# Four engine call lists of a pipelined delta-rule layer laid out in a new order

## The chip, the cores and the metric

The kernel runs on one core of one Trainium2 chip. The metric is the device time of one execution in microseconds. The kernel before takes 4942.76 us, the median of 3 runs (4940.17 to 4954.71). All data is 32-bit floating point.

## The reference

Three layers run one after the other on x of shape (8, 256, 256): a feed-forward layer, an attention layer and a second feed-forward layer. Nearly all of the time is the attention layer (16 heads, 4 keys per token, chunks of 64 tokens in the reference). For every head and chunk:

```python
w = bg[..., None] * kg
M = tril(einsum(k * decay, w), k=-1)              # keys against keys
rhs = vg - einsum('bhtid,bhdv->bhtiv', k * exp(G), S)
u = solve_triangular(M, rhs, lower=True, unit_diagonal=True)
o = scale * (q * exp(G) @ S + einsum(q * decay, w) @ u)
S_new = exp(glast) * S + einsum('bhtid,bhtiv->bhdv', kdec, u)
```

Here q, k and v come from projections of the normalised x, a causal convolution with four taps and a silu; q is normalised over its channels, k through its lengths. G is the running sum of a softplus of a low-rank projection. The output is normalised by its root mean square, gated and projected back.

## The kernel before, in words

The attention layer is cut into 64 steps: 4 blocks of 512 tokens (two sequences each) times 16 heads. The kernel cuts the recurrence into chunks of 32 tokens, so a step has 16 chunks, eight for each of the two sequences. It is a software pipeline written out by hand. A loop variable p runs over periods, and in one period every engine does parts of up to four steps: projections and convolutions of step p, products and masks of step p-1, inverses and the start of the recurrence of step p-2, the rest of the recurrence and the output of step p-3. Each of TensorE (PE), VectorE (DVE), ScalarE (ACT) and GpSimd (POOL) has its own list of calls, which stands in the code in the order in which the engine executes it. Nothing plans this order at run time: an engine takes its next call, waits until the semaphores that the call names have reached their counts, and executes it. So the order of a list is the order of the queue, and a call that waits holds everything behind it.

The calls that matter, by the names in the lists (first argument: the step):

- project_k(s, b) and project_v(s, b) on PE: two 128x512 matrix products each into one of two shared banks. tap_k or tap_v on ACT copies the bank into one of three accumulators, and three calls conv_k or conv_v on DVE (m = 2, 1, 0) add the other taps from the bank and so give it free. silu_k and silu_v on ACT write the result (tiles KQ and V). The tables bank_use and acc_use say which bank or accumulator each use has, and for whose release it waits.
- levels(s, q, l) on DVE writes the scaled keys (tile X) of quarter q of a step at level l from 1 to 4; level(s, q) on POOL does level 0 (tile X0). products(s, q, l) on PE multiplies them with a stationary tile of 128x32. Levels 0 to 2 go to bank 2, levels 3 and 4 to bank 3. When the five products of a quarter are there, evacuate(s, q, 0..3) on DVE (tile Pd, lines 1661 and 1667) and keep(s, q) on ACT (tiles E and At) read them, and only then may products(s, q+1, 0) start.
- take, norm and weigh on DVE prepare the 32x32 diagonal blocks; begin and rows on POOL invert them row by row (tiles LT and LZ, lines 1998 and 2001). unfold and turn on DVE bring the result back (Zc, Ztc), place and shift on ACT lay it into Ztf. first and second on PE use 32x32 tiles, third and fourth 64x64 tiles; with the ACT calls of the same names they build the inverse of a 128x128 chunk. They run twice, once for each half hb of the 16 chunks.
- The recurrence: rhs(s, hb, c) on PE multiplies the state S with kexp; rhs on DVE makes Rs; solve on PE multiplies with the inverse Ztf; solve on ACT copies to Us; update on PE makes the state's change and the chunk's output; update on DVE makes the new S. It goes over c = 0 to 7 for the two sequences hb = 0 and 1, which take turns. The tiles are 128x128.
- The end of a step: out_square and out_root on ACT (tile o) with mean_square on PE between them, gated(s, 0) and gated(s, 1) on DVE, then output on PE and DVE. The bank of the outputs (bank 7) is one for all steps, so update(s, 0, 0) waits for gated(s-1, 1).
- turn(s, q) on PE transposes kdec, a tile that spread(s, q, 0) on POOL writes for one quarter at a time; turn_v(s, q) transposes V. gate, decay, total and mean_square on PE are 128x512 products into the same two shared banks.
- spare(s, j) is empty until the last periods, where units of the second feed-forward layer stand.

PE's list thus changes between tile sizes: 128x128 ("full"), 128x32 (products), 32x32 and 64x64 (inverses). Matrix products of 32-bit numbers show as two instructions each in the trace.

Of the kernel before, what the change touches and what calls it, by code (L numbers as in the profile page):

```python
# [93 lines left out]
def build(nc, x, out, wkq, wv, wo, vec, wf1, wg1, wb, bg1, wu, wd, fvec, wsd, cst, B, H):  # L94
# [6 lines left out]
    with ctx:  # L101
# [580 lines left out]
        v_ck, v_cv, v_sp, v_C = (sem(f"v_{n}") for n in ("ck", "cv", "sp", "C"))  # L682
# [9 lines left out]
        def turns(order, count):  # L692
# [15 lines left out]
            ("vturn", 2, 2, a_vt, 4, 2), ("turn", 0, 1, a_kdT, 4, 0), ("norm", 0, 0, v_max, 1, 0),  # L708
            ("vturn", 3, 2, a_vt, 4, 3), ("turn", 1, 1, a_kdT, 4, 1), ("k", 0, -1, v_ck, 15, 2),
# [3 lines left out]
            ("k", 2, 0, a_k, 5, 2), ("v", 0, 1, a_v, 4, 0), ("v", 1, 1, a_v, 4, 1),  # L713
            ("k", 3, 0, a_k, 5, 3), ("k", 4, 0, a_k, 5, 4), ("v", 2, 1, a_v, 4, 2),
            ("v", 3, 1, a_v, 4, 3), ("k", 0, -1, a_k, 5, 0), ("k", 1, -1, a_k, 5, 1),
# [107 lines left out]
        def delta_tensor(e, ffn):  # L823
# [221 lines left out]
            for p in range(-1, NS + 3):  # L1045
                rhs(p - 3, 0, 3)
                products(p - 1, 0, 1)
                solve(p - 3, 0, 3)
                update(p - 3, 1, 2)
                spare(p - 3, 8)  # L1050
                turn(p - 2, 3)
                update(p - 3, 0, 3)
                rhs(p - 3, 1, 3)
                project_k(p, 2)
                rhs(p - 3, 0, 4)
                solve(p - 3, 1, 3)
                spare(p - 3, 10)
                solve(p - 3, 0, 4)
                update(p - 3, 1, 3)
                spare(p - 3, 11)  # L1060
                update(p - 3, 0, 4)
                rhs(p - 3, 1, 4)
                project_v(p - 1, 0)
                products(p - 1, 0, 2)
                solve(p - 3, 1, 4)
                spare(p - 3, 13)
                rhs(p - 3, 0, 5)
                update(p - 3, 1, 4)
                spare(p - 3, 14)
                solve(p - 3, 0, 5)  # L1070
                products(p - 1, 0, 3)
                rhs(p - 3, 1, 5)
# [7 lines left out]
                products(p - 1, 0, 4)  # L1080
                solve(p - 3, 0, 6)
                rhs(p - 3, 1, 6)
                solve(p - 3, 1, 6)
# [5 lines left out]
                project_v(p - 1, 1)  # L1089
                solve(p - 3, 0, 7)  # L1090
                rhs(p - 3, 1, 7)
                project_k(p, 3)
                solve(p - 3, 1, 7)
                spare(p - 3, 22)
                update(p - 3, 0, 7)
# [13 lines left out]
                project_v(p - 1, 2)  # L1109
                products(p - 1, 2, 0)  # L1110
                products(p - 1, 2, 1)
                project_v(p - 1, 3)
                first(p - 2, 0)
# [4 lines left out]
                products(p - 1, 2, 3)  # L1118
                turn_v(p - 2, 1)
                products(p - 1, 2, 4)  # L1120
# [5 lines left out]
                spare(p - 2, 33)  # L1126
                total(p)
                turn_v(p - 2, 3)
                products(p - 1, 3, 0)
                first(p - 2, 1)  # L1130
                spare(p - 2, 34)
                products(p - 1, 3, 1)
                turn(p - 1, 1)
                second(p - 2, 1)
                spare(p - 2, 35)
                products(p - 1, 3, 2)
                products(p - 1, 3, 3)
                solve(p - 2, 0, 0)
                products(p - 1, 3, 4)
                project_k(p + 1, 0)  # L1140
                third(p - 2, 1)
                spare(p - 2, 36)
                update(p - 2, 0, 0)
                project_k(p + 1, 1)
                fourth(p - 2, 1)
                spare(p - 2, 37)
                rhs(p - 2, 0, 1)
# [4 lines left out]
                spare(p - 2, 2)  # L1152
                update(p - 2, 0, 1)
                rhs(p - 2, 1, 1)
                turn(p - 1, 2)
                rhs(p - 2, 0, 2)
                solve(p - 2, 1, 1)
                spare(p - 2, 4)
                update(p - 2, 1, 1)
                spare(p - 2, 5)  # L1160
                solve(p - 2, 0, 2)
                rhs(p - 2, 1, 2)
                update(p - 2, 0, 2)
                products(p, 0, 0)
                solve(p - 2, 1, 2)
                spare(p - 2, 7)

        def delta_scalar(e, ffn):
# [261 lines left out]
            for p in range(-1, NS + 3):  # L1430
                solve(p - 3, 1, 2)
                factors(p - 1, 3)
                spare(p - 3, 7)
                solve(p - 3, 0, 3)
                turned(p - 2, 2)
                silu_k(p, 0)
                silu_k(p, 1)
                tap_k(p, 2)
                spare(p - 3, 8)
                solve(p - 3, 1, 3)  # L1440
                turned(p - 2, 3)
                spare(p - 3, 10)
                solve(p - 3, 0, 4)
                e.preload_act_table_set("natural_log_exp_and_others")
                length(p - 2, 1)
                factors(p - 1, 4)
                spare(p - 3, 11)
                solve(p - 3, 1, 4)
                tap_v(p - 1, 0)
                factors(p - 1, 5)  # L1450
                spare(p - 3, 13)
                spare(p - 3, 14)
                solve(p - 3, 0, 5)
                solve(p - 3, 1, 5)
                spare(p - 3, 16)
                spare(p - 3, 17)
                solve(p - 3, 0, 6)
                decay(p, 0)
                solve(p - 3, 1, 6)
                above(p)  # L1460
                decay(p, 1)
                silu_k(p, 2)
                tap_v(p - 1, 1)
                spare(p - 3, 19)
# [671 lines left out]
```

How the kernel before makes its waits and increments, by code:

```python
    def wait_ge(self, sem, n):  # L74
        if n > self.stood.get(sem.name, 0):
            self.stood[sem.name] = n
            self.e.wait_ge(sem, n)
# [142 lines left out]
            def load():  # L220
                if NU:
                    w.wait_ge(p_k, every(NS - 1, 5))
                    w.wait_ge(p_v, every(NS - 1, 4))
                    w.wait_ge(p_decay, every(NS - 1, 1))
                    w.wait_ge(p_gate, every(NS - 1, 1))
                e.dma_start(f.fv[:, :], fvec).then_inc(f.d_fv, 16)
                for i in range(2):
                    if i + 1 < NT or not NU:
                        load_x(i)
                e.dma_start(f.wuh[:, :, :], wuh_d).then_inc(f.d_wu[0], 16)
                if NU:
                    w.wait_ge(a_k, every(NS - 1, 5))
                    w.wait_ge(a_v, every(NS - 1, 4))
                e.dma_start(f.wdh[:, :, :], wdh_d).then_inc(f.d_wd, 16)
# [1 line left out]
            def load_x(n):  # L236
                if n < NT:
                    if not f.first:
                        w.wait_ge(d_x2[n % 2], 16 * (n // 2 + 1))
                    e.dma_start(f.xt[:, n % 2], f.src[n]).then_inc(f.d_x[n % 2], 16)
# [1 line left out]
            def store(n):  # L242
                if f.first and n:
                    store_low(n - 1)
                w.wait_ge(*f.emptied[f.place["down", n, 3]])
                e.dma_start(f.dst[n], f.x1[:, n % 2]).then_inc(f.d_o[n % 2], 16)
# [66 lines left out]
            def fold_up(n):  # L313
                w.wait_ge(f.d_wu[0], 32)
                w.wait_ge(f.s_fly, 2 * n + 2)
                for a in range(2):
```

## Time and profile before

| what | value |
|---|---|
| median of 3 runs | 4942.76 us |
| the profiled execution | 4954.81 us, its span 4952.9 us |
| PE, DVE, ACT, POOL busy | 91%, 84%, 69%, 65% of the span |
| mean granted TensorE clock | 0.98 |
| starts of out_square | 64, from 428.4 us to 4861.3 us |

The two feed-forward layers and the filling and emptying of the pipeline lie before 428 us and after some 4560 us. Between stand 60 periods of the steady state. Their lengths, from one out_square to the next, add up to 4134.9 us: 27 of the 60 are between 67.3 and 68.3 us, the others between 68.3 and 71.6 us. Busy shares do not tell what bounds such a pipeline, since each engine waits for the others in turn. It is read from the chain of waits through one period, and from what each engine does in its parts.

### The profile page before, as it was taken

What the parts mean: (1) busy time and instruction counts of PE and PEld (TensorE: products, weight loads), DVE (VectorE), ACT (ScalarE), POOL (GpSimd) and SP (SyncE); (2) the same over time, 40 slices, a digit from 0 to 9 for tenths busy, and PEclk for the clock granted to TensorE, in tenths of its full rate; (3) what the DMA queues carried; (4) which work ended last, traced back from release to release, by engine and by line L of the source; (5) the groups of instructions that cost most, each with busy time, mean ns of one, the idle gap of its engine ahead of it and who ended that gap; (6) DMA issues with size and microseconds to landing.
All of it is one profiled execution on the core that took longest, in us unless ns stands there. A gap on an engine that the chain in (4) does not pass through costs nothing.

```text
span 4952.9 us, 151365 instructions
## 1 busy us (share of the span) xinstructions
PE 4487.4 (91%) x63200; PEld 3133.3 (63%) x63200; DVE 4148.3 (84%) x7262; ACT 3394.4 (69%) x6708; POOL 3198.9 (65%) x5316
## 2 busy tenths in 40 slices
PE   8869999999999999999999999999999999999888
PEld 5536666666666666666666666666666666666655
DVE  3279999989999999999989999899999899999622
ACT  3267777777777777777777777777777777777531
POOL 0047777776777777777767777677777777677600
PEclk9989999999999999999999999999999999999799
DMA  2200000000000000000100000000000000000100
GB/s 87 88 26 24 26 25 25 15 24 25 34 32 18 25 25 26 25 15 24 34 32 30 15 24 26 25 25 14 30 30 25 25 14 25 26 25 9 37 9 22
DMA packets 49723, 135.45 MB, mean 27 GB/s; under 512 B 7056, under 2 KB 28176, under 8 KB 48400
## 3 DMA queue, kind: packets, MB, share of 16 engines
q1 hardware_dynamic: 49040, 125.77, 7.2%
q8 instruction: 498, 8.16, 0.7%
q14 instruction: 185, 1.52, 0.1%
HBM read 111.60 MB, written 14.16 MB: 25 GB/s over the span
## 4 chain that ended last, share of the span: by engine, by line
PE 57%; DVE 27%; ACT 8%; issue 6%; POOL 1%; DMA 0%; DVEq 0%; SPq 0%; ACTq 0%
PE bank L835 48%; DVE acc L1556 8%; PE bank L302 7%; DVE X L1553 7%; DVE sp_t L1553 2%; ACT o L1182 2%; PE bank L906 2%; DVE o L1556 2%; DVE Rs L1556 2%; DVE Pd L1661 1%; ACT L1471 1%; DVE Zc L1740 1%; DVE x1m L1553 1%; ACT Ztf L1181 1%; ACT rn L1182 1%
## 5 line engine op out<-in xcount | busy, mean ns | idle before, releaser
L1556 DVE SCALAR_TENSOR_TENSOR acc<-bank,vc,acc 128x510 f32<-128x510 f32 (+2 forms) x1728 | 1271.6, 739 | 124.5 <-ACT acc L1181 98.9
L2001 POOL TENSOR_TENSOR LZ<-LZ,LT 128x120 f32<-128x120 f32 (+26 forms) x1984 | 935.0, 471 | 155.5
L1553 DVE TENSOR_TENSOR X<-KQ,Fl 128x640 f32<-128x640 f32 x1024 | 1019.3, 1011 | 0.6 <-ACT Fl L1182 0.6
L1998 POOL TENSOR_TENSOR LT<-LA,LZ 128x120 f32<-128x120 f32 (+26 forms) x1984 | 921.0, 464 | 145.8
L1971 POOL COPY X<-KQ 128x640 f32<-128x640 f32 x256 | 249.2, 973 | 874.8 <-DVE KQ L1553 279.2
L835 PE MATMUL bank<-X 128*32 128x60 f32 (+1 forms) x32768 | 653.3, 206 | 136.2 <-DVE Pd L1661 85.9
L835 PEld LDWEIGHTS bank<-X 128*32 128x32 f32 x32768 | 527.3, 112 | 363.3 <-issue 205.6
L1181 ACT ACTIVATE Us<-bank 128x128 f32<-128x128 f32 x1024 | 282.4, 277 | 641.2 <-PE bank L835 630.2
L835 PE MATMUL bank<-xnTm,WK 128*128 128x512 f32 x1280 | 638.2, 623 | 42.1 <-DVE acc L1556 36.4
L1950 POOL TENSOR_TENSOR kdec<-KQ,Fe 128x512 f32<-128x512 f32 x256 | 337.4, 1318 | 303.8 <-PE bank L906 303.8
L835 PE MATMUL bank<-Rs,Ztf 128*128 128x128 f32 x2048 | 469.5, 315 | 68.1 <-DVE Rs L1556 48.0
L835 PE MATMUL bank<-xnTm,WV 128*128 128x512 f32 x1024 | 496.4, 607 | 12.7 <-ACT sg L1182 4.8
L1556 DVE SCALAR_TENSOR_TENSOR Rs<-V,knT,bank 128x128 f32<-128x128 f32 x896 | 308.2, 344 | 190.4 <-PE bank L835 181.6
L835 PEld LDWEIGHTS bank<-Rs,Ztf 128*128 128x128 f32 x2048 | 318.6, 191 | 197.7 <-DVE Rs L1556 114.5
L1181 ACT ACTIVATE acc<-bank,vc 128x512 f32<-128x512 f32 x576 | 393.8, 684 | 65.9 <-PE bank L835 63.5
L835 PE MATMUL bank<-Us,kdT 128*128 128x128 f32 x1792 | 400.4, 306 | 38.3 <-ACT Us L1181 23.6
L835 PE MATMUL bank<-S,kexp 128*128 128x128 f32 x1792 | 389.0, 299 | 9.1 <-DVE S L1556 5.8
L835 PEld LDWEIGHTS bank<-xnTm,WK 128*128 128x128 f32 x1280 | 225.0, 196 | 269.8 <-issue 166.7
L1950 POOL TENSOR_TENSOR kexp<-KQ,Fe 128x512 f32<-128x512 f32 x256 | 387.4, 1524 | 0.0
L835 PE MATMUL bank<-qn,S 128*128 128x32 f32 x1792 | 350.1, 278 | 0.0
L835 PEld LDWEIGHTS bank<-S,kexp 128*128 128x128 f32 x1792 | 283.3, 193 | 85.5 <-issue 35.5
L835 PEld LDWEIGHTS bank<-Us,kdT 128*128 128x128 f32 x1792 | 273.2, 192 | 90.4 <-ACT Us L1181 76.8
(144 smaller groups left out, 9267.3 us busy)
## 6 DMA issues: line engine op xcount, KB each, us to landing
WK<-in_wkq SPq DMA_DIRECT2D x64, 704.0 KB, 6.0
WV<-in_wv SPq DMA_DIRECT2D x64, 576.0 KB, 3.8
WO<-in_wo SPq DMA_DIRECT2D x64, 128.0 KB, 2.0
wuh<-in_wu SPq DMA_DIRECT2D x2, 1024.0 KB, 7.4
xt<-in_x SPq DMA_DIRECT2D x4, 512.0 KB, 6.3
wuh_d<-wuh SPq DMA_DIRECT2D x1, 2048.0 KB, 6.3
x_d<-x SPq DMA_DIRECT2D x4, 512.0 KB, 3.0
xnT_d<-xT SPq DMA_DIRECT2D x4, 512.0 KB, 2.7
```

Source lines behind the costliest of these rows:

```text
L302: return e.matmul(o, l, r, start=start, stop=stop, skip_group_check=True)
L835: return e.matmul(o, l, r, start=start, stop=stop, skip_group_check=True)
L906: ins = e.transpose(o[:, P * c:P * c + P], kdec[:, c, :], ident)
L1181: return e.activation(o, i, f, scale=scale)
L1182: return e.activation(o, i, f, bias=bias, scale=scale)
L1471: e.preload_act_table_set("natural_log_exp_and_others")
L1553: return e.tensor_tensor(o, a, b, op)
L1556: return e.scalar_tensor_tensor(out=o, in0=a, scalar=sc, in1=b, op0=op0, op1=op1)
L1950: return e.tensor_tensor(o.rearrange("p u (g i t) -> p (u g) i t", g=4, i=R), kq[:, 16 * q:16 * q + 16, 0:R, :], f.unsqueeze(2).broadcast_ ...
L1971: e.tensor_copy(X0[:, :, 0:40], kk.rearrange("p g i t -> p g (i t)")).then_inc(g_copy, 1)
L1998: e.tensor_tensor(tmp, LA[:, j + 1:32, 8 * (j % R) + j // R].unsqueeze(2).broadcast_to([P, rr, cc]), LZ[:, j, 0:cc].unsqueeze(1).broadcast ...
L2001: e.tensor_tensor(LZ[:, j + 1:32, 0:cc], LZ[:, j + 1:32, 0:cc], tmp, SUB).then_inc(g_row, 1)
```

## The change

All calls stay, and each handles the same data with the same instruction. What changes is their order in the four lists, and with it the two tables that hand out banks (two entries change places) and accumulators (none does). PE's list has 97 calls in a period, DVE's 109, ACT's 85, POOL's 21. The diff's core, which is PE's list from the start of a period to its first outputs:

```diff
                 rhs(p - 3, 0, 3)
-                products(p - 1, 0, 1)
+                update(p - 3, 1, 2)
                 solve(p - 3, 0, 3)
...
-                project_v(p - 1, 0)
-                products(p - 1, 0, 2)
...
                 solve(p - 3, 0, 5)
+                products(p - 1, 0, 2)
                 products(p - 1, 0, 3)
...
+                update(p - 3, 0, 7)
                 project_k(p, 3)
...
-                mean_square(p - 3)
-                project_k(p, 4)
                 products(p - 1, 1, 0)
                 products(p - 1, 1, 1)
+                mean_square(p - 3)
                 products(p - 1, 1, 2)
+                project_k(p, 4)
+                output(p - 3, 0)
                 products(p - 1, 1, 3)
                 products(p - 1, 1, 4)
-                output(p - 3, 0)
```

Counted over a period of the list, PE changes its tile size 37 times before and 34 times now.

The first place is PE after the key products of the last quarter of a step have begun (step p-1) and while the second half of the inverses is made (step p-2). X are key products, Ztf with kexp and kdec tiles of 128x128, Zc and Y inverse products, WK the projections. Before, from products(3, 3) on:

```order
L835 MATMUL bank<-X 32x40 x8
L835 MATMUL bank<-Rs,Ztf 128x128
L835 MATMUL bank<-X 32x80 x8
L835 MATMUL bank<-xnTm,WK 128x512 x2
L835 MATMUL bank<-Zc,E 64x64 x8
L835 MATMUL bank<-Us,kdT 128x128
L835 MATMUL bank<-At,Us 128x32
L835 MATMUL bank<-xnTm,WK 128x512 x2
L835 MATMUL bank<-Ztf,Y 64x64 x8
L835 MATMUL bank<-S,kexp 128x128
L835 MATMUL bank<-Rs,Ztf 128x128 x2
```

Now, from project_k(p+1, 0) on, which stands right behind second(p-2, 1):

```order
L835 MATMUL bank<-xnTm,WK 128x512 x2
L835 MATMUL bank<-Rs,Ztf 128x128
L835 MATMUL bank<-Zc,E 64x64 x8
L835 MATMUL bank<-Us,kdT 128x128
L835 MATMUL bank<-At,Us 128x32
L835 MATMUL bank<-Ztf,Y 64x64 x8
L835 MATMUL bank<-S,kexp 128x128
L835 MATMUL bank<-xnTm,WK 128x512 x2
L835 MATMUL bank<-Rs,Ztf 128x128 x2
```

The two key products no longer stand around the first solve (they come ahead of second now, side by side), and project_k(p+1, 1) has moved from before fourth (Ztf,Y) to behind it and behind the first rhs.

The second place is PE at the end of a step's recurrence and the start of its output; o is the output tile. Before, from rhs(p-3, 0, 7):

```order
L835 MATMUL bank<-S,kexp 128x128
L835 MATMUL bank<-xnTm,WV 128x512 x2
L835 MATMUL bank<-Rs,Ztf 128x128
L835 MATMUL bank<-S,kexp 128x128
L835 MATMUL bank<-xnTm,WK 128x512 x2
L835 MATMUL bank<-Rs,Ztf 128x128
L835 MATMUL bank<-At,Us 128x32
L835 MATMUL bank<-qn,S 128x32
L835 MATMUL bank<-At,Us 128x32
L835 MATMUL bank<-qn,S 128x32
L835 MATMUL bank<-o,cs 128x512
L835 MATMUL bank<-xnTm,WK 128x512 x2
```

Now, from project_v(p-1, 1), the row behind the same rhs:

```order
L835 MATMUL bank<-xnTm,WV 128x512 x2
L835 MATMUL bank<-S,kexp 128x128
L835 MATMUL bank<-Rs,Ztf 128x128 x2
L835 MATMUL bank<-At,Us 128x32
L835 MATMUL bank<-qn,S 128x32
L835 MATMUL bank<-xnTm,WK 128x512 x2
L835 MATMUL bank<-At,Us 128x32
L835 MATMUL bank<-qn,S 128x32
L835 MATMUL bank<-X 32x60 x16
L835 MATMUL bank<-X 32x20 x16
L835 MATMUL bank<-o,cs 128x512
L835 MATMUL bank<-X 32x20 x16
```

project_k(p, 3) now stands between the last two updates, and key products surround mean_square (o,cs).

The third place is ACT at the same time; acc are the taps, E and At belong to keep, o to the output, rn to the decay of step p. Before:

```order
L1181 ACTIVATE acc<-bank,vc 128x512
L1182 ACTIVATE o<-bank 128x512
L1471 ACT_TABLE_LOAD
L1182 ACTIVATE rn<-rn,cs 128x512
L1182 ACTIVATE o<-bank,cs 128x512
L1182 ACTIVATE o<-o 128x512
L1181 ACTIVATE E<-bank 128x384
L1181 ACTIVATE At<-bank 128x4x24
```

Now:

```order
L1181 ACTIVATE acc<-bank,vc 128x512
L1181 ACTIVATE E<-bank 128x384
L1181 ACTIVATE At<-bank 128x4x24
L1182 ACTIVATE o<-bank 128x512
L1473 ACT_TABLE_LOAD
L1182 ACTIVATE o<-bank,cs 128x512
L1182 ACTIVATE o<-o 128x512
L1182 ACTIVATE rn<-rn,cs 128x512
```

keep(p-1, 0) has moved ahead of out_square, and the decay's logarithm behind the two roots. On DVE, levels(p-1, 1, 4) now stands between query and gated, lengths(p-2) has moved to just ahead of the levels of quarter 2, and unfold and turn stand one evacuation earlier. In the last quarter levels 3 and 4 come ahead of add_up. On POOL, level(p-1, 1) has moved two groups of rows back, and the first kdec comes before the last two calls of level.

## Rows read from the trace of the kernel before

**Rows 1.** The page: busy shares, and the shares of the last chain.

```profile
PE 4487.4 (91%) x63200; PEld 3133.3 (63%) x63200; DVE 4148.3 (84%) x7262; ACT 3394.4 (69%) x6708; POOL 3198.9 (65%) x5316
PE 57%; DVE 27%; ACT 8%; issue 6%; POOL 1%; DMA 0%; DVEq 0%; SPq 0%; ACTq 0%
```

**Rows 2.** Chain of waits, one period: start us, us, what.

```profile
2353.24 0.60 ACT o L1182
2353.86 1.28 ACT L1471
2355.15 0.72 ACT rn L1182
...
2357.93 0.75 DVE o L1556
...
2421.37 0.60 ACT o L1182
```

**Rows 3.** PE timeline, one period's waits: start us, us, operation, idle before and releaser.

```profile
2378.08 0.63 PE L835 MATMUL bank<-X 128*32 128x60 f32 x32 [1.43 <-DVE Pd L1661]
...
2382.39 0.75 PE L835 MATMUL bank<-X 128*32 128x80 f32 x16 [0.38 <-DVE X L1553]
...
2390.24 0.93 PE L835 MATMUL bank<-Rs,Ztf 128*128 128x128 f32 x4 [0.26 <-ACT Ztf L1181]
```

**Rows 4.** Busy time by stretch: the window, its length, each engine's busy us.

```profile
2347.63:2358.68 11.05, 9.55 (x114) 5.33 (x117) 9.21 (x19) 9.45 (x16) 9.48 (x21) 1.00 0.01 2
2358.68:2378.08 19.40, 17.60 (x346) 11.74 (x337) 19.05 (x31) 15.63 (x29) 12.94 (x18) 1.00 0.26 90
2378.08:2390.24 12.16, 11.52 (x261) 8.00 (x261) 12.02 (x18) 10.18 (x22) 4.91 (x4) 1.00 0.01 3
2390.24:2415.76 25.52, 24.27 (x270) 19.62 (x271) 22.55 (x47) 15.70 (x36) 22.72 (x42) 1.00 0.01 2
```

**Rows 5.** PE in a long period: a stall.

```profile
2449.88 0.22 PE L835 MATMUL bank<-Ztf,Ys 32*32 32x32 f32 x2 [0.91 <-issue]
```

**Rows 6.** PE busy in a stretch of 0.4 us: length, busy, granted clock.

```profile
2450.40:2450.80 0.40, 0.40 (x34) 0.50 0.00 0
```

**Rows 7.** PE timeline: neighbours of equal and of different tile size.

```profile
2397.19 0.39 PE L835 MATMUL bank<-S,kexp 128*128 128x128 f32 x2
2397.51 0.45 PE L835 MATMUL bank<-X 128*32 128x20 f32 x32
...
2400.29 1.88 PE L835 MATMUL bank<-xnTm,WK 128*128 128x512 f32 x4
2402.01 0.38 PE L835 MATMUL bank<-S,kexp 128*128 128x128 f32 x2
2402.23 0.39 PE L835 MATMUL bank<-Rs,Ztf 128*128 128x128 f32 x2
2402.84 0.49 PE L835 MATMUL bank<-Rs,Ztf 128*128 128x128 f32 x2 [0.22 <-DVE Rs L1556]
```

**Rows 8.** ACT timeline: the last tap before out_square, and keep behind it.

```profile
2352.42 0.68 ACT L1181 ACTIVATE acc<-bank,vc 128x512 f32<-128x512 f32 x1
...
2357.08 0.47 ACT L1181 ACTIVATE E<-bank 128x384 f32<-128x384 f32 x1
```

**Rows 9.** DVE timeline: softplus and levels beside POOL's kdec and kexp; levels alone.

```profile
2374.30 1.75 DVE L1553 TENSOR_TENSOR sp_t<-sp_t,rn 128x512 f32<-128x512 f32 x1
2375.98 1.89 DVE L1553 TENSOR_TENSOR X<-KQ,Fl 128x640 f32<-128x640 f32 x1
...
2378.66 0.78 DVE L1553 TENSOR_TENSOR X<-KQ,Fl 128x640 f32<-128x640 f32 x1
```

**Rows 10.** POOL timeline: first row of a step's inverses, and the last.

```profile
2392.89 0.25 POOL L1998 TENSOR_TENSOR LT<-LA,LZ 128x31 f32<-128x31 f32 x1
...
2429.50 0.22 POOL L2001 TENSOR_TENSOR LZ<-LZ,LT 128x16 f32<-128x16 f32 x1
```

**Rows 11.** DVE timeline: unfold, which waits for POOL's last row.

```profile
2431.05 1.17 DVE L1740 STREAM_TRANSPOSE Zc<-LZ 128x256 f32<-128x256 f32 x2
```

More of the change, by code:

```diff
@@ L1143, in delta_tensor @@
                 update(p - 2, 0, 0)
+                fourth(p - 2, 1)
+                rhs(p - 2, 0, 1)
+                spare(p - 2, 37)
                 project_k(p + 1, 1)
-                fourth(p - 2, 1)
-                spare(p - 2, 37)
-                rhs(p - 2, 0, 1)
                 solve(p - 2, 1, 0)
@@ L1152, in delta_tensor @@
                 spare(p - 2, 2)
+                turn(p - 1, 2)
+                rhs(p - 2, 1, 1)
                 update(p - 2, 0, 1)
-                rhs(p - 2, 1, 1)
-                turn(p - 1, 2)
+                solve(p - 2, 1, 1)
                 rhs(p - 2, 0, 2)
-                solve(p - 2, 1, 1)
                 spare(p - 2, 4)
-                update(p - 2, 1, 1)
+                products(p, 0, 0)
                 spare(p - 2, 5)
                 solve(p - 2, 0, 2)
+                update(p - 2, 1, 1)
                 rhs(p - 2, 1, 2)
                 update(p - 2, 0, 2)
-                products(p, 0, 0)
+                spare(p - 2, 7)
                 solve(p - 2, 1, 2)
-                spare(p - 2, 7)
         def delta_scalar(e, ffn):
@@ L1476, in delta_scalar @@
                 out_root(p - 3, 1)
-                keep(p - 1, 0)
+                decay(p, 2)
                 tap_k(p, 4)
+                silu_v(p - 1, 1)
+                silu_k(p, 3)
                 keep(p - 1, 1)
-                silu_k(p, 3)
-                silu_v(p - 1, 1)
+                silu_k(p, 4)
                 gate_out(p - 1)
@@ L1805, in delta_vector @@
             for p in range(-1, NS + 3):
-                conv_k(p, 1, 1)
-                spare(p - 3, 7)
                 rhs(p - 3, 0, 3)
                 conv_k(p, 1, 0)
-                levels(p - 1, 0, 2)
                 update(p - 3, 1, 2)
                 distance(p - 1, 4)
+                levels(p - 1, 0, 1)
                 spare(p - 3, 8)
+                levels(p - 1, 0, 2)
+                rhs(p - 3, 1, 3)
                 update(p - 3, 0, 3)
+                distance(p - 1, 5)
+                update(p - 3, 1, 3)
@@ L1826, in delta_vector @@
                 update(p - 3, 0, 4)
-                levels(p - 1, 0, 4)
-                spare(p - 3, 13)
+                update(p - 3, 1, 4)
                 rhs(p - 3, 0, 5)
                 levels(p - 1, 1, 1)
-                update(p - 3, 1, 4)
+                spare(p - 3, 13)
+                rhs(p - 3, 1, 5)
+                spare(p - 3, 14)
                 conv_k(p, 2, 0)
-                spare(p - 3, 14)
-                rhs(p - 3, 1, 5)
+                update(p - 3, 0, 5)
+                levels(p - 1, 1, 2)
@@ L1846, in delta_vector @@
                 update(p - 3, 0, 6)
-                levels(p - 1, 1, 3)
-                evacuate(p - 1, 0, 0)
+                diagonal(p - 2)
                 update(p - 3, 1, 6)
                 spare(p - 3, 20)
+                evacuate(p - 1, 0, 0)
                 rhs(p - 3, 0, 7)
-                levels(p - 1, 1, 4)
+                levels(p - 1, 1, 3)
+                evacuate(p - 1, 0, 1)
+                rhs(p - 3, 1, 7)
                 conv_v(p - 1, 1, 2)
-                rhs(p - 3, 1, 7)
+                spare(p - 3, 22)
@@ L1875, in delta_vector @@
                 output(p - 3, 1)
-                evacuate(p - 1, 1, 3)
                 unfold(p - 2, 0)
@@ L1879, in delta_vector @@
                 turn(p - 2)
+                evacuate(p - 1, 1, 3)
+                lengths(p - 2)
                 levels(p - 1, 2, 1)
```

227 lines of the change are left out of this document (110 added, 117 removed).

## The prediction

> **What bounds the kernel now.** I read the busy shares first: PE 91%, DVE 84% [rows 1], so neither is full, and the last chain changes engines (PE 57%, DVE 27%, ACT 8%). So I took the chain of waits through one period [rows 2]. It starts at out_square (2353.24), runs on ACT and DVE to the end of gated(1) at 2358.68, stays on DVE to the start of products(p-1, 3, 0) at 2378.08 [rows 3], and from there on it is mostly PE until the next out_square at 2421.37. That period is 68.13 us. I name four points: G, gated(1) ends; U, products(3, 0) starts; S, solve(p-2, 1, 0) starts; Y, rhs(·, 0, 7) starts. The period is then four stretches [rows 4]: Y to G 11.05 us, G to U 19.40, U to S 12.16, S to the next Y 25.52. The reader is to see in the busy times which engine fills each: DVE 19.05 of 19.40 between G and U, PE 24.27 of 25.52 between S and Y; in Y to G no engine is full, since it is a chain of latencies. PE's larger waits [rows 3] are 1.43 us before U (for DVE's masks), 0.38 for DVE's levels and 0.26 for the inverse.
>
> The 60 steady periods take 4134.9 us, 68.9 on average, so 48 us above 60 x 68.13. In long periods PE stalls without a named releaser (0.91 us, [rows 5]) and then runs at a granted clock of 0.50, which is the lower level, 1.2 GHz [rows 6]. I carry these 48 us over unchanged; a rival below does not.
>
> **Fewer changes of tile size.** A full-tile product is followed by the next of its size after 0.22 us (2402.01 to 2402.23) and by a key product after 0.32 (2397.19 to 2397.51) [rows 7]: 0.10 us for a change. Changing back I price alike, as an estimate. Three changes fewer in a period are 0.3 us, at most 20 us in all, and only where PE is the bound. Two of the joins lie there (products(0, 2) beside (0, 3); (3, 3) and (3, 4) around no solve), worth 0.2 us each with both changes; the new entries around mean_square and output lie where PE waits anyhow. The Trainium skill (TensorEngine Tiling (Array Packing), Key Properties) says that a change of tiling mode drains the engine; TensorE: Matmul & The Clock Gate (Step-by-step) puts the drain at about 128 cycles. At 2.4 GHz that would be an estimate of 0.05 us a change and 10 us in all: by both it is a small term.
>
> What decides is the order. I walked the new lists through the four stretches with the durations of this period, each call starting at the latest of its engine's last call and what it waits for. A hop of the recurrence is some 0.8 us: rhs starts on PE at 2402.01, Rs comes back from DVE and solve starts at 2402.84 [rows 7]. Solve to update, through Us on ACT, and update to rhs, through S on DVE, are as long.
>
> **Y to G: +0.5 us.** Two things move. The good one: the decay's logarithm (0.72 us, [rows 2]) no longer stands between out_square and the roots. The bad ones: project_k(3), 1.7 us (2400.29 to 2402.01 for such a call, [rows 7]), now sits between update(0, 7) and update(1, 7), and out_square stands on ACT behind tap_k(3) (0.68) and keep(0) (0.6 for its two calls) [rows 8]. tap_k(3) can only start when project_k(3) is through, about when update(1, 7) starts; so ACT reaches out_square 0.7 us after the last update instead of at once. On DVE evacuate(0, 1) and levels(1, 3) now come before rhs(1, 7), which costs PE another 0.4, and on PE products(1, 0) now needs evacuate(0, 3), which is ready just when PE gets there. Sum: -0.72 for the logarithm, +0.75 for out_square, +0.4 for rhs, +0.1 for levels(1, 4), which has just moved in front of gated. Bounds: -0.7 if tap and keep hide, +1.4 if the evacuation is also late and mean_square with it.
>
> **G to U: +0.8 us.** DVE is full here, so every change counts whole. products(1, 3) and (1, 4) now run after output(0), which waits for gated; evacuate(1, 0) follows three taps (2.2 us) after G, but output(0), 1.2, and the two products, 1.1, are ready at 2.4 with the bank's latency: 0.3 us of waiting. lengths comes in: 0.15. POOL runs its first kdec and level(2) while DVE does the levels of quarter 2; such a DVE call takes up to 1.89 us beside kdec and kexp and 0.78 alone [rows 9]. I take 0.35 for a partial overlap (0 to 1.1). PE stays ahead of DVE: its wait before U shrinks from 1.43 to about 1.
>
> **U to S: -0.9 us.** PE is the bound in the second half. products(3, 3) and (3, 4) have their levels earlier, since add_up (1.2 us) moved behind them: the wait of 0.38 goes, with one pair of changes, 0.2. Then project_k(p+1, 1), 1.8 us, stands between fourth and solve(1, 0), so ACT copies the inverse beside it and the wait of 0.26 goes; fourth itself now waits 0.1 to 0.3 for Y, which had been hidden behind the projection. Behind a waiting fourth stands the whole recurrence, so this counts. 11.25 us by the walk. Bounds: 0 (if ACT, which has root, length, the first factors and fourth in a row there, is 0.9 late) and -1.2.
>
> **S to Y: -0.6 us.** PE's own work is some 23.2 of the 25.52 us, and 23.0 in the new order with one pair of changes fewer. The rest is waiting for Rs, S and Us. In the new order I find waits of 0.37 at the start, 0.45 at turn(3) (kdec, because rows starts 0.7 later after S on POOL), 0.5 at update(1, 3), 0.3 at solve(0, 5), 0.2 at solve(0, 6) and some small ones: 1.9 us, so 24.9. products(0, 1) gives up its place between rhs and solve of chunk 3 for one in chunk 4 that fills a gap. Bounds: +0.6 (DVE holds two more taps or levels in front of an rhs, 0.7 each) and -1.3.
>
> **The sum.** 0.5 + 0.8 - 0.9 - 0.6 = -0.2 us in a period; over 60 periods -12 us. A walk leaves out collisions, but the three terms on DVE and ACT were also each taken at their full cost. The first layer does not change; in the last periods only the order of units and recurrence does, nothing that I can price: 0, between -5 and +5. Against the profiled execution that is 4954.8 - 12 = 4943; it lies 12 us above the median of the runs, so against the median it is 4931. That is the forecast.
>
> **Rivals.** (1) The stretches Y to G and G to U don't get longer. For it: the logarithm's 0.72 is a real row on the chain; POOL has idle time there; PE's wait of 1.43 before U shows that PE could take the moved products for nothing. Against it: DVE is full between G and U. Then U to S and S to Y would count alone, -1.5 us. POOL cuts that: it inverts from 2392.89 to 2429.72 with hardly a gap [rows 10], and unfold starts 1.3 us later, at 2431.05 [rows 11]. In the walk POOL starts no earlier after U than before, and unfold stands 0.3 us further ahead of the next U, so a period can lose about 1.0 us: 60 x -1.0 = -60, 4883.
>
> (2) Slower: out_square held on ACT. Place: ACT between solve(1, 7) and gated. Mechanism: tap_k(3), keep(0), out_square, its table load (1.28) and both roots are one row behind project_k(3), and DVE with its 19 full microseconds is behind them. Whatever makes project_k(3) late (an Us held on ACT, the bank) is now paid there in full, while before only update(1, 7) stood ahead of out_square. If also evacuate(0, 3) is late for products(1, 0), mean_square passes the table load. Price: the upper bounds of the first two stretches, +1.4 and +1.1 (against my 0.5 and 0.8), less the same 1.5: +1.0 in a period, 60 us, 5003; half of the way, 4973. It decides from the point where the first two stretches together lose more than 1.5 us. For it: four reorderings meet in this place, all towards a later G. Against it: ACT is busy 9.45 of 11.05 us there and 15.63 of 19.40 behind it [rows 4], so it can catch up.
>
> (3) The long periods go or multiply. The stall of rows 5 and the low clock come in the stretch U to S, soon after the wait before U; with that wait down to 1 us the clock might stay at 2.4 GHz more often. All 48 us gone gives 4943 - 48 = 4895 with the sum at zero; a third more of them gives 4959. The Trainium skill (TensorE: Matmul & The Clock Gate, The HAM clock gate) ties the lower clock to an idle engine; this trace agrees in that the low clock follows a wait and a stall.
>
> (4) The new order does nothing measurable, because DVE's total (62.83 of 68.13 us) and the recurrence stay: 4943.
>
> **How the numbers follow.** A change under 0.3% (15 us) can't be told from none here. Forecast, a slight gain about 4931 (own range 4905 to 4955): 0.38, of it faster by over 0.3% 0.18, same 0.15, slower 0.05. Rival 1: 0.22. Rival 2: 0.22. Rival 3: 0.10, of it 0.07 faster and 0.03 slower. Rival 4: 0.08, of it 0.06 same and 0.02 slower. Together faster 0.47, same 0.21, slower 0.32. The range reaches to both sides, from rival 1 to somewhat beyond half of rival 2: 4870 to 4990.
>
> **What would show it.** In the profile after: the same four stretches, about 11.6, 20.2, 11.3 and 24.9 us. Y to G: out_square starts some 0.7 us after the last product of update(1, 7), behind At. G to U: a wait of DVE for PE before the first evacuation of quarter 1, and PE's wait before products(3, 0) nearer 1 us. U to S: no wait before solve(1, 0), a short one before fourth. S to Y: turn(3) waits for kdec. The prediction is wrong if G to U stays at 19.4 (then rival 1), if out_square comes 1.5 us or more after the last update (rival 2), or if the recurrence, S to Y, is longer than 25.5 us.

## The result

| kernel | median us | range, runs | profiled execution: time, span, clock |
|---|---|---|---|
| before | 4948.74 | 4940.17 to 4957.55, 4 | 4954.81, 4952.9, 0.98 |
| changed | 5039.84 | 5022.75 to 5047.97, 4 | 5022.75, 5021.0, 0.95 |

The ratio is 1.0179, 95% interval 1.0145 to 1.0214: the change makes the kernel 91 us slower. The forecast was 4931 and the range 4870 to 4990, so the time lies outside, on the other side. In all that follows, one execution alone is far off: one of ten of the old lists with late loads took 7244.86 us at a mean granted clock of 0.54, and its ratio leaves that one out.

The page of the changed kernel, its busy shares and its last chain:

```profile
PE 4541.9 (90%) x63200; PEld 3239.2 (65%) x63200; DVE 3923.5 (78%) x7262; ACT 3388.3 (67%) x6709; POOL 3070.7 (61%) x5316
PE 68%; DVE 11%; ACT 10%; issue 7%; POOL 3%; DMA 0%; SPq 0%; DVEq 0%; POOLq 0%; ACTq 0%
```

Against [rows 1], DVE has 225 us less to do for the same instructions, PE 55 us more, and the chain went from DVE (27% to 11%) to PE (57% to 68%). So something became cheaper on DVE and something dearer on PE. Both can be seen by taking periods apart.

**An undisturbed period is 2.3 us shorter.** The four stretches of one, in the form of [rows 4]:

```profile
2460.98:2472.75 11.77, 9.90 (x128) 5.59 (x127) 10.38 (x19) 8.75 (x15) 10.44 (x21) 1.00 0.01 1
2472.75:2490.60 17.85, 17.08 (x313) 11.51 (x313) 17.18 (x30) 14.79 (x29) 12.18 (x20) 1.00 0.40 127
2490.60:2502.55 11.95, 11.16 (x261) 8.27 (x261) 10.33 (x18) 10.71 (x24) 4.56 (x4) 1.00 0.01 4
2502.55:2526.78 24.23, 23.62 (x272) 19.53 (x270) 21.63 (x44) 16.34 (x39) 21.54 (x42) 1.00 0.01 2
sum 65.80, PE 61.76 PEld 44.90 DVE 59.52 ACT 50.59 POOL 48.71; mean PE 15.44 PEld 11.23 DVE 14.88 ACT 12.65 POOL 12.18
```

The sum is 65.80 us against 68.13 (a short stall of 0.71 us between U and S is in it), and DVE is busy 59.52 us of it against 62.83. The second stretch, G to U, gave most: 17.85 against 19.40. DVE and POOL timelines of its end, to be read beside [rows 9]:

```profile
2487.28 0.68 DVE L1553 TENSOR_TENSOR sp_t<-sp_t,rn 128x512 f32<-128x512 f32 x1
...
2488.41 1.75 DVE L1553 TENSOR_TENSOR X<-KQ,Fl 128x640 f32<-128x640 f32 x1
```

```profile
2488.20 1.27 POOL L1950 TENSOR_TENSOR kdec<-KQ,Fe 128x512 f32<-128x512 f32 x1 [1.68 <-PE bank L906]
2489.42 1.87 POOL L1950 TENSOR_TENSOR kexp<-KQ,Fe 128x512 f32<-128x512 f32 x1
```

Softplus took 1.75 us before, beside kdec; now it is through before kdec starts and takes 0.68.

**But most periods are disturbed.** The 60 steady periods add up to 4208.1 us (4134.9 before). So against 60 of its own good ones the changed kernel loses 4208.1 - 60 x 65.80 = 260 us, the kernel before lost 4134.9 - 60 x 68.13 = 47. The good periods give 2.33 x 60 = 140 us, the bad ones take 213 more: +73 us, and the two profiled spans differ by 68.1, since the period behind these is 4.5 us shorter. (The medians of the runs differ by more, 91 us.) What such a loss looks like on PE, from the end of project_v(3) on:

```profile
2545.61 1.88 PE L835 MATMUL bank<-xnTm,WV 128*128 128x512 f32 x4
2547.42 0.63 PE L835 MATMUL bank<-X 128*32 128x60 f32 x32
2548.27 0.69 PE L835 MATMUL bank<-Zc,E 32*32 32x32 f32 x32 [0.21 <-ACT Ztf L1181]
2548.89 0.74 PE L835 MATMUL bank<-X 128*32 128x20 f32 x64
...
2554.97 1.34 PE L835 MATMUL bank<-X 128*32 128x40 f32 x19 [4.34 <-issue]
```

PE stops in the middle of a key product, products(2, 3), of which 13 instructions have run and 19 follow 4.34 us later. It can't wait for a tile there, and no releaser is named. The stretches around it (length, busy times, granted clock, DMA share, GB/s):

```profile
2549.40:2551.40 2.00, 1.23 (x87) 1.03 (x75) 1.97 (x3) 1.03 (x3) 2.00 (x3) 1.00 0.99 375
2551.40:2553.40 2.00, 0.00 (x0) 0.00 (x0) 0.77 (x2) 0.09 (x1) 0.90 (x1) 0.78 0.80 271
2553.40:2555.40 2.00, 0.43 (x10) 0.43 (x12) 0.00 (x0) 0.00 (x0) 0.00 (x0) 0.50 0.07 18
2555.40:2557.40 2.00, 2.00 (x19) 1.45 (x16) 1.03 (x3) 0.00 (x1) 0.00 (x0) 0.50 0.04 8
2557.40:2563.40 6.00, 6.00 (x42) 5.43 (x43) 2.00 (x6) 3.84 (x8) 2.16 (x2) 0.50 0.00 0
```

The DMA engines are full when it stops, at 2550.63. The granted clock falls to its lower level (0.50, 1.2 GHz) at 2552.50, while PE stands still, and stays there until 2566.15, through some 11 us of work. Over the 60 periods the clock is low for 338 us, against 51 before, and PE's stalls without a releaser add up to 147 us against 50: 97 of the 213 us are standstill, and the other 116 go with the 287 us more at the low clock. The DMA queues (queue, kind: packets, MB, share of 16 engines), first for 2548 to 2552.5, then for 2552.5 to 2553:

```profile
q1 hardware_dynamic: 391, 1.42, 86.2%
...
q1 hardware_dynamic: 67, 0.06, 50.6%
q8 instruction: 1, 0.02, 11.8%
```

q1 moves the weights WV (576 KB) and WK (704 KB) of step s+2, which SP issues as soon as project_v(3) has freed WV's buffer (at 2547.57, and WK at 2548.00). q8 brings instructions, in packets of 16 KB. The page has its sum, the same for both kernels:

```profile
q8 instruction: 498, 8.16, 0.7%
```

8.16 MB for PE's 126,400 products and weight loads and the 1,191 instructions of its sequencer in the trace are 64 bytes each, so I read q8 as PE's own supply, with an estimated 256 instructions in a packet. From 2547.57, when the weights start, no such packet comes until 2552.66; PE resumes at 2554.97, 2.3 us after it starts. The kernel before has the same transfers behind its project_v(3). They were survived, since PE needed fewer instructions there. First the kernel before, for 3.1 us from the issue of WV's load, then the changed one from the issue to the stop:

```profile
2368.54:2371.64 3.10, 2.95 (x144) 2.55 (x142) 3.00 (x5) 2.74 (x8) 3.10 (x4) 1.00 0.70 221
```

```profile
2547.50:2550.60 3.10, 2.88 (x189) 2.52 (x189) 3.06 (x5) 2.04 (x5) 2.45 (x3) 1.00 0.64 221
```

286 instructions (matrix products and weight loads) in 3.1 us there, and 335 in the whole 5 us of the transfer; 378 in 3.1 us here, and more were due.

One stall could be chance; the starts of all q8 packets say more. Of the changed kernel's 73 stalls of over 0.25 us, 72 end 2.2 to 3.1 us after a packet starts, though packets start only every 10 us (the median). And if PE's instructions (its sequencer's own among them) are counted and the packets numbered by 256, a packet starts when PE is 150 to 415 instructions beyond its number in the kernel before. In the changed kernel 28 of 449 packets start only at 449, the same count each time, wherever PE is in its list; it has stopped by then and goes on 2.2 to 2.7 us later. No packet starts at 449 before, none with the late loads and one with the small ones of the experiments. So the packet comes too late, and it is the transfers that make it so late.

The waits of PE without a releaser at L835, 428 to 4524 us (in total, times, longest), of before and after:

```profile
PE bank L835 <- issue: 44.9, 93, 1.8
```

```profile
PE bank L835 <- issue: 128.0, 67, 4.9
```

### The profile page after: what moved, and what is told of

The parts are those of the page before. It is cut to its first block, busy times and chain, and to the rows that moved or that the text cites. A ratio compares the mean times of both kernels' runs of the same rounds, so it can differ in the third digit from the quotient of the medians.

```text
span 5021.0 us, 151305 instructions
## 1 busy us (share of the span) xinstructions
PE 4541.9 (90%) x63200; PEld 3239.2 (65%) x63200; DVE 3923.5 (78%) x7262; ACT 3388.3 (67%) x6709; POOL 3070.7 (61%) x5316
## 3 DMA queue, kind: packets, MB, share of 16 engines
q8 instruction: 498, 8.16, 0.7%
## 4 chain that ended last, share of the span: by engine, by line
PE 68%; DVE 11%; ACT 10%; issue 7%; POOL 3%; DMA 0%; SPq 0%; DVEq 0%; POOLq 0%; ACTq 0%
PE bank L835 55%; PE bank L302 7%; DVE acc L1556 6%; PE bank L897 3%; ACT Ztf L1181 3%; PE bank L906 3%; ACT acc L1181 3%; DVE rn L1553 1%; ACT Us L1181 1%; POOL LT L1998 1%; ACT sg L1182 1%; DVE Pd L1661 1%; POOL LZ L2001 1%; ACT Fl L1182 1%; ACT V L1181 1%
## 5 line engine op out<-in xcount | busy, mean ns | idle before, releaser
L1998 POOL TENSOR_TENSOR LT<-LA,LZ 128x120 f32<-128x120 f32 (+26 forms) x1984 | 941.3, 474 | 147.3 <-issue 1.5
L1553 DVE TENSOR_TENSOR X<-KQ,Fl 128x640 f32<-128x640 f32 x1024 | 874.4, 874 | 1.4 <-ACT Fl L1182 1.4
L835 PEld LDWEIGHTS bank<-X 128*32 128x32 f32 x32768 | 536.2, 114 | 391.9 <-issue 260.5
L835 PE MATMUL bank<-X 128*32 128x60 f32 (+1 forms) x32768 | 650.5, 208 | 143.9 <-issue 71.7
L1971 POOL COPY X<-KQ 128x640 f32<-128x640 f32 x256 | 203.2, 794 | 842.4 <-issue 339.6
L1950 POOL TENSOR_TENSOR kdec<-KQ,Fe 128x512 f32<-128x512 f32 x256 | 351.0, 1371 | 554.3 <-PE bank L906 547.8
L835 PE MATMUL bank<-xnTm,WK 128*128 128x512 f32 x1280 | 630.2, 616 | 12.7 <-DVE acc L1556 7.0
L835 PE MATMUL bank<-xnTm,WV 128*128 128x512 f32 x1024 | 481.7, 603 | 13.3 <-ACT sg L1182 9.2
L835 PE MATMUL bank<-Rs,Ztf 128*128 128x128 f32 x2048 | 449.2, 307 | 30.1 <-DVE Rs L1556 29.2
L835 PEld LDWEIGHTS bank<-Rs,Ztf 128*128 128x128 f32 x2048 | 319.2, 191 | 163.1 <-issue 62.3
L835 PE MATMUL bank<-Us,kdT 128*128 128x128 f32 x1792 | 390.3, 300 | 26.4 <-ACT Us L1181 1.5
L835 PE MATMUL bank<-S,kexp 128*128 128x128 f32 x1792 | 377.4, 299 | 4.6
L835 PE MATMUL bank<-qn,S 128*128 128x32 f32 x1792 | 348.5, 277 | 0.0
L835 PEld LDWEIGHTS bank<-Us,kdT 128*128 128x128 f32 x1792 | 276.9, 192 | 104.3 <-ACT Us L1181 62.3
L835 PEld LDWEIGHTS bank<-xnTm,WK 128*128 128x128 f32 x1280 | 222.6, 193 | 182.4 <-issue 163.3
L835 PEld LDWEIGHTS bank<-At,Us 128*128 128x128 f32 x2048 | 317.8, 193 | 29.9 <-issue 29.2
L1950 POOL TENSOR_TENSOR kexp<-KQ,Fe 128x512 f32<-128x512 f32 x256 | 335.0, 1319 | 0.0
```

The lines of the kernel that those rows point to most:

```text
L835: return e.matmul(o, l, r, start=start, stop=stop, skip_group_check=True)
L1553: return e.tensor_tensor(o, a, b, op)
L1950: return e.tensor_tensor(o.rearrange("p u (g i t) -> p (u g) i t", g=4, i=R), kq[:, 16 * q:16 * q + 16, 0:R, :], f.unsqueeze(2).broadcast_ ...
L1971: e.tensor_copy(X0[:, :, 0:40], kk.rearrange("p g i t -> p g (i t)")).then_inc(g_copy, 1)
L1998: e.tensor_tensor(tmp, LA[:, j + 1:32, 8 * (j % R) + j // R].unsqueeze(2).broadcast_to([P, rr, cc]), LZ[:, j, 0:cc].unsqueeze(1).broadcast ...
```

## The experiments

Theory T: the long stalls come where the transfers of WV and WK meet a row of small products, which needs many instructions. Rival D: the row of small products, joined together by the new order, runs out of instructions by itself. Both count a stall and the low clock behind it. "Stalls" below are those of over 0.25 us without a releaser in mid-program; before has 98 with 50.3 us, most of it in two places (16.8 us ahead of products(1, 0), 20.8 us between U and S), the changed kernel 73 with 146.2 us, 119.6 of them at 18 to 23 us after out_square, right behind project_v(3). The 16.8 us are of another kind: 0.29 us in nearly every period, with no packet near. Without them the supply cost the kernel before 34 us, and the changed one 145. The ratio is to the kernel before, run beside it (medians 4952.50 to 4957.31 us).

**Late loads, new lists.** In SP's list both loads wait on:

```diff
+                        w.wait_ge(p_sol, nth(p - 2, 16, 3))
                         load_wv(s + 2)
...
+                    w.wait_ge(p_sol, nth(p - 2, 16, 3))
                     load_wk(s + 2)
```

> The new lists, with the loads of the next WV and WK (576 and 704 KB) held back on the DMA queue until solve(p-2, 1, 1), that is until the recurrence, where TensorE has few instructions per microsecond. Theory T (transfers): in the changed kernel these loads start right behind project_v(3), now just ahead of the densest row of key and inverse products, and TensorE's instructions arrive late beside them; the stall then brings the low clock. T expects no stall of 4 us near 20 us into a period, periods of 65.8 to 67 us nearly throughout, clock 0.98 or more, and 5040 - 60 x 5 = about 4740 to 4790 us. Rival D (density): the joined small products outrun the instruction supply by themselves. D expects stalls and time as in the changed kernel, 5020 to 5050 us.

4821.09 us, ratio 0.9735 (0.9709 to 0.9762). Stalls 66.2 us. The largest single step, 219 us off, and D's forecast falls; but T's own was passed by 31 us, and 37 us of stalls stay at the old place.

**Small loads, new lists.** From step 2 on only 32 columns of each weight are loaded, so most projections work with old weights; the instructions are the same.

```diff
+                c = 11 * P if s < 2 else 32
-                e.dma_start(WK[:, s % 2, :], wkq[s % H]).then_inc(d_wk[s % 2], 16)
+                e.dma_start(WK[:, s % 2, 0:c], wkq[s % H][:, 0:c]).then_inc(d_wk[s % 2], 16)
... (WV alike)
```

> The new lists; from the third step on only 32 of the columns of WK and WV are loaded (32 KB each), so the weights of the first two heads stay in use: the large transfers are left out, nothing waits in another place. T expects the same as with the loads held back, 4740 to 4790 us. D expects 5020 to 5050 us. If this one is fast and the late loads are slow, the transfers hurt wherever they lie.

4836.32 us, ratio 0.977 (0.9734 to 0.9807), stalls 66.1 us. (The expectation's 32 KB are 16 KB each in the trace.) With hardly any data moving, 203 us go, about as many as with late loads, and not the 250 or more of T's forecast. What is left behind project_v(3), 37 us in 30 places, is not the transfers' doing. D is right about a part.

**Loads at U, old lists.** The opposite: the loads are held until products(3, 0) may start, so they meet the small products between U and S.

```diff
+                        w.wait_ge(v_Pd, nth(p - 1, 16, 11))
                         load_wv(s + 2)
...
+                    w.wait_ge(v_Pd, nth(p - 1, 16, 11))
                     load_wk(s + 2)
```

> The old lists, with the loads of WV and WK held until evacuate(p-1, 2, 3), so that they run beside products(3, 0) and what follows, the old order's own dense part. T expects stalls of TensorE without a named releaser there, more long periods, a mean clock of 0.96 or less, and 5000 us or more. D expects no change, 4940 to 4960 us.

5069.52 us, ratio 1.0231 (1.0206 to 1.0257), stalls 106 us, 65 of them at 30 to 34 us after out_square; 19 packets start at a count of 449. T's forecast holds, but for the clock (0.97, not 0.96 or less). The kernel before gets the fault of the changed one by its loads alone.

**Only project_v(3) back, new lists.** One call of PE's list goes back to where it was, and first(p-2, 0) and products(2, 1) change places with it:

```diff
                 project_v(p - 1, 2)
-                project_v(p - 1, 3)
                 products(p - 1, 2, 0)
-                first(p - 2, 0)
                 products(p - 1, 2, 1)
+                project_v(p - 1, 3)
+                first(p - 2, 0)
```

> The new lists, with only project_v(p-1, 3) on TensorE put back behind products(2, 0) and (2, 1) as before. The load of WV then starts 0.8 us later and 64 of the small products lie ahead of it. T expects part of the loss back, 4880 to 4990 us. D expects 5020 to 5050 us, since only one change of tile size is moved and the four small groups behind it stay together.

4773.36 us, ratio 0.9634 (0.9614 to 0.9654), stalls 50 us. Faster than both kernels and than either theory allowed. The mean period is 66.14. The edit both delays the weights (by 1.0 us) and breaks the row of small products with 1.9 us of large ones, so it weakens both causes. It doesn't part them, nor the move of first from that of project_v(3); the next run moves project_v(3) alone.

**Only project_v(3) forward, old lists.**

```diff
+                project_v(p - 1, 3)
                 products(p - 1, 2, 0)
                 products(p - 1, 2, 1)
-                project_v(p - 1, 3)
```

> Old lists in everything, except that project_v(3) stands on PE ahead of products(2, 0) and (2, 1), where the new lists have it. If the place of project_v(3) is what made the changed kernel slow (by starting the weight loads ahead of the dense small products and by joining these into one row), the old lists lose by it too: 5010 to 5060 us, PE's stalls of over 0.25 us rise from 50 to over 90 us, some 18 to 22 us after out_square. Rival (the loss needs the whole new order, and this call's place only matters in it): 4940 to 4975.

5117.56 us, ratio 1.0338 (1.0304 to 1.0372), stalls 122 us, 67 of them at 18 to 23 us; 18 packets start at a count of 449. That is slower than the 5010 to 5060 expected. This single line costs the old lists 164 us. It doesn't need the rest of the new order.

**Old lists, project_v(3) forward, late loads.**

> Old lists with project_v(3) ahead of products(2, 0), and the loads of WV and WK held until the third product of solve. It completes a square: in the new lists, late loads took 219 us off with project_v(3) forward and 9 us with it back; in the old ones with it back, nothing. If the long stalls need both (loads in flight, and a row of small products behind project_v(3) without a large one between): 4965 to 5010 us, that is over 100 us off the 5118 of the same lists with early loads, with a rest of 15 to 50 us against the old kernel for the density alone. If density alone does it in the old lists: 5080 to 5120.

4975.9 us, ratio 1.0045 (1.0026 to 1.0064). As expected: 142 of the 164 us go with the loads, 22 stay.

**Late loads, old lists; and new lists with project_v(3) back.** The same two waits.

> Old lists, with only the loads of WV and WK held until the third product of solve. The old lists have 50 us of PE's stalls without a releaser, in two places: 21 us some 28 us after out_square, where the loads land, and 17 us some 4 us after it, with no load. Theory T: the first place nearly goes, the second stays; the steady periods come from 68.9 to 68.3 us and the time to 4905 to 4930. Rival D (loads do not matter in the old lists): 4940 to 4960.

4948.9 us, ratio 0.9998 (0.9981 to 1.0015): nothing. T's forecast (4905 to 4930) fails and D's holds. The stalls between U and S, which I had put down to the loads, stay at 19 us.

> New lists with project_v(3) back behind products(2, 1), and the loads of WV and WK held until the third product of solve, as in the run with late loads. The run with only project_v(3) back took 4773 us and still lost 35 of its 50 us of PE's stalls without a releaser some 26 to 28 us after out_square, where its weight loads now land, and its steady periods average 66.2 us against 65.4 at best. Theory T (stalls come where weight loads and many small PE instructions meet): these stalls fall below 15 us and the time to 4735 to 4760. Rival D (the density of the small products alone makes them): the stalls stay, 4765 to 4785.

4764.75 us, ratio 0.9627 (0.9608 to 0.9647): at best 9 us, which the intervals can't tell from none, and the stalls at 25 to 29 us only fall from 39 to 29. The time lies between the two forecasts; the stalls (under 15 us by T) are D's. The square is then (medians of series run apart, us; the kernel before took up to 4957 beside them):

| | loads at once | loads late |
|---|---|---|
| new lists, project_v(3) forward (the change) | 5040 | 4821 |
| new lists, project_v(3) back | 4773 | 4765 |
| old lists, project_v(3) forward | 5118 | 4976 |
| old lists, project_v(3) back (before) | 4949 | 4949 |

Loads cost 219 and 142 us where the small products follow project_v(3) directly, and 0 to 9 where they don't. With late loads the place of the call is still worth 56 and some 25 us: the density of the row alone (in the 56, the place of first is included). So both theories hold a part: nearly all of the loss needs transfers and a dense row together, and a dense row alone makes the rest.

**POOL's order back.** New lists with project_v(3) back; in POOL's list spread(p-1, 0, 0) stands behind level(p-1, 3) again.

> New lists with project_v(3) back; on POOL the first kdec of a step stands again behind the last two calls of level, as in the old list. This moves kdec and kexp by 1.3 us to later, so that they lie beside DVE's softplus and levels of the last quarter. Theory C (the stretch from gated to products(3, 0) is shorter in the new order because DVE's tensor_tensor calls no longer meet POOL's kdec and kexp): softplus takes 1.2 to 1.8 us in place of 0.68, the period is 0.5 to 1.2 us longer, 4805 to 4845 us. Rival (DVE's gain comes from elsewhere, or PE hides it): 4765 to 4785.

4775.32 us, ratio 0.965 (0.963 to 0.9669): no difference, softplus 0.685 us (the median over mid-program is 1.76 in the kernel before and 0.68 in the changed one). My theory C, as put there, falls: the second kdec waits for turn(0) on PE, wherever the first one stands.

**Softplus back.** The same kernel; DVE's softplus stands behind two evacuations again:

```diff
                 levels(p - 1, 3, 1)
-                softplus(p)
                 spare(p - 2, 32)
                 evacuate(p - 1, 2, 1)
                 evacuate(p - 1, 2, 2)
+                softplus(p)
                 levels(p - 1, 3, 2)
```

> New lists with project_v(3) back; on DVE softplus stands again behind evacuate(2, 1) and (2, 2), right ahead of levels(3, 2), as in the old list. POOL's order alone did not bring the meeting of softplus with kdec back (the run with POOL's old order: softplus 0.685 us and no difference in time), since the second kdec waits for turn(0) on PE. Here softplus starts 0.5 to 0.7 us later, when kdec runs. Theory C2 (the gain of the stretch up to products(3, 0) comes from softplus standing ahead of POOL's second kdec): softplus takes 1.5 to 1.8 us, levels(3, 2) is late by as much, periods grow by 0.5 to 1.1 us, 4800 to 4840 us. Rival (DVE has the slack, PE is the bound there now): 4765 to 4785.

4820.62 us, ratio 0.9731 (0.9716 to 0.9746), 47 us slower than without this edit; undisturbed periods are mostly 66.65 us in place of 65.5. (The mean period grows less, from 66.13 to 66.91 us, since the stalls fall from 50 to 25 us.) DVE, POOL and PE there:

```profile
1919.17 1.68 DVE L1553 TENSOR_TENSOR sp_t<-sp_t,rn 128x512 f32<-128x512 f32 x1
1920.78 1.88 DVE L1553 TENSOR_TENSOR X<-KQ,Fl 128x640 f32<-128x640 f32 x1
```

```profile
1919.03 1.27 POOL L1950 TENSOR_TENSOR kdec<-KQ,Fe 128x512 f32<-128x512 f32 x1 [2.54 <-PE bank L906]
1920.26 1.72 POOL L1950 TENSOR_TENSOR kexp<-KQ,Fe 128x512 f32<-128x512 f32 x1
```

```profile
1922.86 1.21 PE L835 MATMUL bank<-X 128*32 128x60 f32 x96 [1.36 <-DVE Pd L1661]
```

Softplus starts 0.14 us after kdec and ends 0.55 us after it; levels start 0.52 us after kexp and end 0.68 us after it: each DVE call seems to do its 0.7 us of work behind the POOL call. kexp itself takes 1.72 us where it took 1.25 with no such DVE call in front. And PE's wait of 1.4 us before products(3, 0) [rows 3] is back. The Trainium skill (SBUF — State Buffer, Who interferes with whom) says that a VectorE instruction with two SBUF inputs and a GpSimd one that reads SBUF block each other whole, the later one until the first is through; these rows agree.

**A large product into the second row.** The stalls left lie between U and S. From new lists, project_v(3) back, late loads:

```diff
                 turn(p - 1, 1)
+                project_k(p + 1, 0)
                 spare(p - 2, 35)
                 products(p - 1, 3, 3)
                 products(p - 1, 3, 4)
                 second(p - 2, 1)
-                project_k(p + 1, 0)
                 solve(p - 2, 0, 0)
```

> As the best run so far (new lists, project_v(3) back, late loads: 4765 us), with project_k(p+1, 0), two 128x512 products of 1.8 us together, moved from behind second(p-2, 1) to ahead of products(3, 3). The stalls that are left, 27 us in 33 places some 26 us after out_square, lie in the row products(3, 0) to second(1), which has no large product between. If the length of such a row makes them: under 10 us of stalls there, 4735 to 4760 us, unless the later levels and masks cost it back. Rival (the stalls come from something else, or second(1) and what waits for it is now 1.8 us late): 4765 to 4830.

4945.96 us, ratio 0.9989 (0.9977 to 1.0002), 181 us slower. The stalls did go, to 7 us, as expected; the time did not follow, and lies far outside the rival's forecast too. Nearly all periods are 68.7 to 69.6 us. PE's waits there, and the granted clock before, in and after them:

```profile
1836.30 1.14 PE L837 MATMUL bank<-Zc,E 64*64 64x64 f32 x16 [0.86 <-ACT Ztf L1183]
1838.04 0.46 PE L837 MATMUL bank<-Us,kdT 128*128 128x128 f32 x2 [0.60 <-ACT Us L1183]
```

```profile
1829.30:1835.44 6.14, 6.14 (x219) 4.48 (x218) 4.23 (x7) 4.46 (x8) 4.06 (x3) 1.00 0.01 3
1835.44:1839.46 4.02, 2.56 (x35) 2.41 (x36) 3.88 (x7) 3.87 (x10) 0.00 (x0) 1.00 0.01 4
1839.46:1842.87 3.41, 3.41 (x10) 1.79 (x9) 3.34 (x8) 2.44 (x8) 1.84 (x3) 0.50 0.00 0
```

project_k had covered the way from second through ACT to third. Without it PE is busy only 2.56 of 4.02 us, and behind that it works at the lower clock, in 51 of the 60 periods. Most of the nine periods without the low clock are 66.3 us, against 65.5 with project_k where it was and 68.7 or more with the low clock; so the waits cost some 0.8 us and the clock 2.4 or more.

**A short one.** The same start; turn(p-1, 1), 0.66 us, goes from behind first(p-2, 1) to between products(3, 1) and (3, 2).

> As the best run so far (new lists, project_v(3) back, late loads: 4765 us), with turn(p-1, 1), four 128x128 transposes of 0.66 us together, moved from behind first(p-2, 1) to between products(3, 1) and (3, 2). If a short full-size call is enough to let the instructions catch up wherever it stands, it makes no difference, since the row is split now too, only elsewhere: 4755 to 4775. If it must be long, the same. Only if the stalls hang on how many small instructions follow the wait ahead of products(3, 0) does it gain: 4740 to 4755.

4762.28 us, ratio 0.9622 (0.9592 to 0.9653): no difference that can be told from 4764.75. The stalls at that place fall from 29 to 23 us.

## Why the prediction was wrong

**The step that failed is "I carry these 48 us over unchanged".** I had seen the stall without a releaser and the low clock behind it [rows 5, 6], and counted them as a fixed sum. They are a product of the order: of how many small instructions stand in a row, and of what the DMA engines do meanwhile. They rose from 47 us (my 48) to 260. Rival 3 had named this loss, stall and low clock together, but with the wrong size ("a third more", 16 us), place and cause: it tied it to the wait before U, which did shrink, while the loss grew at the other place, behind project_v(3). I priced project_v(3)'s move at nothing, without a reason. It frees WV's buffer, and so starts 1.3 MB of transfers; the loads are issued by SP, whose list isn't in the diff. The square shows this: 5040 with the loads at once, 4821 with them late, and a further 56 us by the call's place.

**The errors partly cancel.** My sum was -12 us over 60 periods. An undisturbed period gained 2.33 us and not 0.2, which is 128 us better than the sum; the disturbed ones lost 213 us more than the nothing that I gave them. The difference is the +73 against -12 of the profiled executions. Had the second error been half as large, the time would have come out near the forecast by luck.

**Tile-size changes** stayed small in the forecast, 20 us at most, and no run isolates them. What was shown is that joining small products can cost more than it saves: the row that the new order put together is the one that stalls, and with project_v(3) back in it, one change of tile size more, the kernel is 267 us faster.

**The four stretches** (predicted, measured): Y to G 11.6, 11.77. G to U 20.2, 17.85. U to S 11.3, 11.95, of which 0.71 is a stall without a releaser, so 11.24 without it. S to Y 24.9, 24.23. Three are within their bounds, S to Y just so; G to U is wrong in sign. I had allowed +0.35 us for POOL's calls beside DVE's and had not seen that softplus moves ahead of the second kdec. Put back alone (in the lists with project_v(3) back) it costs 1.15 us in a good period, against the 1.55 gained. Rival 1's sign was right there, its size too small, and its reason (the logarithm) not the one: Y to G was longer, as forecast.

**Its signs in the profile.** out_square starts at 2467.61, right behind At, as written. PE's wait before products(3, 0) was to shrink to 1 us; it is gone in the period shown. fourth does not show a wait, nor turn(3) one for kdec, in this period.

**Rival 2** had the sign of the result, but not its way: ACT does not hold G up by more than was priced (11.77 us).

What stays open: why periods of the same order differ (65.4 to 68 us with project_v(3) back). A period has some 1977 of PE's products and loads [rows 4], 7.7 packets by the estimate above, so a packet falls at another point of it each time; that fits, but no run moved that point alone. Open too is what the 0.29 us ahead of products(1, 0) waits for.

## What to carry to other kernels

An engine's stall without a releaser in a row of many small instructions can be the instruction supply. It is if the stall ends a fixed time after an instruction packet starts (here 2.2 to 3.1 us); stalls with no packet near are something else. Look at what the DMA queues do in the microseconds before it, and keep large transfers away from such rows, or put long instructions in between that cover some useful latency. When a call moves, ask which buffer it frees and what another queue issues then. Check the length of disturbed and undisturbed periods apart: this change made every good period 2.3 us shorter and lost by the others, and one call moved back (with first behind it) made it 3.7% faster than before.

## What was not expected of the hardware

While weights passed at 315 to 375 GB/s no packet of PE's instructions came for 5.1 us, and PE, which had used 378 instructions in 3.1 us, stood still until 2.3 us after the start of the next one. With hardly any such transfer a row of small products still stalls for 1.2 us on average now and then (37 us in 30 places). And a granted clock of 0.50 followed 2.56 busy of 4.02 us in 51 of 60 periods, at a cost (2.4 us or more) some three times that of the waits themselves.
